# A cross-attention kernel: the softmax division leaves the probabilities and is done once per batch on the outputs

## The reference, cut to what matters

```python
def _L0_xattn_ref(query, context, Wq, bq, Wkv, bkv, Wout, bout):   # query (16, 64, 512), context (16, 1601, 512)
    q = query @ Wq + bq
    kv = context @ Wkv + bkv                       # interleaved k and v
    ...                                            # 16 heads of 32
    scores = jnp.einsum('bhid,bhjd->bhij', q, k) * SCALE
    attn = jax.nn.softmax(scores, axis=-1)
    out = jnp.einsum('bhij,bhjd->bhid', attn, v)
    return out.reshape(B, LQ, H * D) @ Wout + bout

x = x + _L0_xattn_ref(_layernorm(x), ctx_1024, ...)
x = x + _L0_attn_ref(_layernorm(x), ...)           # linear attention over the 64 rows of a batch
x = x + _L0_ffn_ref(_layernorm(x), ...)            # top 2 of 8 experts
```

## Time and profile before

| | us |
|---|---|
| median of 3 runs | 2648.12 |
| lowest and highest run | 2643.91, 2648.58 |
| the profiled execution: span from first to last instruction | 2643.8 |

### The profile page before, as it was taken

How to read it: one execution, slowest core, us unless ns; L and a number is a source line. 1 busy time by engine, 2 the same in 40 slices (tenths; PEclk the granted TensorE clock), 3 DMA queues, 4 the chain that set the end, 5 groups by cost and what they waited for, 6 DMA issues and landing times. The chain is left out here.

```text
span 2643.8 us, 41258 instructions
## 1 busy us (share of the span) xinstructions
PE 2413.4 (91%) x14596; PEld 2125.1 (80%) x14596; DVE 1749.9 (66%) x2316; ACT 1099.2 (42%) x1878; POOL 1081.5 (41%) x436
## 2 busy tenths in 40 slices
PE   8899999999999999999999999998579928999994
PEld 6688888888888888888888888886438628999993
DVE  3177777777778787777777777778764425554552
ACT  3244444444444454444444444444322214444440
POOL 2155555555455554545545555554320021111113
PEclk9999999999999999999999999999889959999997
DMA  4211111111111111111111111113030033443433
GB/s 149 90 29 45 37 45 41 54 43 38 38 49 43 35 57 37 38 52 33 53 45 37 39 46 54 39 42 102 8 142 1 1 123 136 148 157 141 167 123 119
DMA packets 114016, 176.91 MB, mean 67 GB/s; under 512 B 51856, under 2 KB 71568, under 8 KB 113808
## 3 DMA queue, kind: packets, MB, share of 16 engines
q1 hardware_dynamic: 108048, 159.51, 19.2%
q0 software_dynamic: 2560, 8.39, 1.0%
q10 hardware_dynamic: 3200, 6.29, 0.6%
HBM read 137.19 MB, written 36.96 MB: 66 GB/s over the span
## 5 line engine op out<-in xcount | busy, mean ns | idle before, releaser
L356 POOL TENSOR_TENSOR k_parts<-k_t,k_parts 64x1602 fp32r<-64x1602 f32 x128 | 426.0, 3328 | 458.1 <-DVE k_parts L418 458.0
L646 PE MATMUL ps_kv<-ctx_hi,wk_hi 128*128 128x256 f32 (+1 forms) x1536 | 464.0, 302 | 13.0 <-POOL ctx_lo L345 13.0
L646 PE MATMUL ps_kv<-ctx_lo,wk_hi 128*128 128x256 f32 (+1 forms) x1536 | 441.1, 287 | 0.0
L646 PE MATMUL ps_kv<-ctx_hi,wk_lo 128*128 128x256 f32 (+1 forms) x1536 | 440.6, 287 | 0.0
L370 POOL TENSOR_TENSOR v_parts<-v,v_parts 128x832 fp32r<-128x832 f32 x128 | 281.4, 2199 | 381.1 <-ACT v_parts L581 379.9
L451 DVE TENSOR_SCALAR probs_both<-probs_both,row_inv 128x1601 f32<-128x1601 f32 x128 | 407.4, 3183 | 4.5
L646 PE MATMUL ps_kv<-wv_hi,ctx_hi 128*128 128x512 f32 (+1 forms) x832 | 340.1, 409 | 0.0
L646 PE MATMUL ps_kv<-wv_hi,ctx_lo 128*128 128x512 f32 (+1 forms) x832 | 327.8, 394 | 0.0
L646 PE MATMUL ps_kv<-wv_lo,ctx_hi 128*128 128x512 f32 (+1 forms) x832 | 326.7, 393 | 0.0
L551 ACT ACTIVATE k_t<-ps_kv,bk_sb 128x256 f32<-128x256 f32 (+1 forms) x384 | 185.8, 484 | 306.3 <-PE ps_kv L646 301.7
L458 DVE TENSOR_TENSOR probs_t<-ps_pt,probs_t 128x512 fp32r<-128x512 f32 x368 | 205.9, 559 | 153.7 <-ACT probs_t L563 150.4
(11 more groups left out here) (215 smaller groups left out, 4219.2 us busy)
## 6 DMA issues: line engine op xcount, KB each, us to landing
w_raw<-w_dram SPq DMA_DIRECT2D x96, 512.0 KB, 4.8
ctx_raw<-ctx_dram SPq DMA_DIRECT2D x81, 512.0 KB, 3.6
rows_in<-zeros SPq DMA_DIRECT2D x90, 128.0 KB, 2.0
ctx_raw<-ctx_dram SPq DMA_DIRECT2D x16, 644.0 KB, 4.2
q_blocks<-q_parts SPq DMA_DIRECT2D x256, 32.0 KB, 1.8
rows_out<-zeros SPq DMA_DIRECT2D x1, 6144.0 KB, 21.2
rows<-rows_in SPq DMA_DIRECT2D x8, 768.0 KB, 5.7
rows_out<-down ACTq DMA_DIRECT2D x8, 768.0 KB, 3.6
```

The costliest lines, as they stand in the source:

```text
L356: nc.gpsimd.tensor_tensor(k_parts[64 - 64 * s:128 - 64 * s, :], k_t[par][64 * s:64 * s + 64, g, :], k_parts[64 * s:64 * s + 64, :].bitcast ...
L646: last = nc.tensor.matmul(o, still, moving, start=(k == 0 and i == 0), stop=(k == DT - 1 and i == 2))
```

## The change: what it does

- `normalise` is replaced by `invert`: DVE still takes the reciprocal of each row's sum, now kept for all eight pairs of a batch (`row_inv` is 128 x 2 x 8), and the multiplication of the 128x1601 probabilities is gone. Turn 0 waits for exp (`exp_done`) in place of the product.
- The outputs are then sums of undivided exponentials. `outputs` adds the four parts with one reduction over the lower 64 rows and two additions that read `ps_o` directly. `o_t` is 128 x 4 x 128: the pair's 64 rows by both heads' 64 columns; only the blocks in which head and rows agree are used. The turned and the values' matmuls now wait for `o_done`, the end of outputs, not for the reductions.
- Once per batch, at p = 0 of the next one, `divide` multiplies `o_t` by the inverse sums and adds the bias, two DVE operations of 128x512. The inverse sums stand as one number per partition (query), and are needed along the free axis: SP writes them to DRAM (`inv_t`, one transfer of single 4-byte elements), waits for it, and reads them back in four transfers that repeat each row over 32 partitions (`spread_inv`, at p = 7 behind `load_q`).
- The output is stored in four transfers in place of one (`store_o`), behind `o_final`.
- The score row stands centred in its four banks, at columns 222 to 1823: the column groups are 290, 512, 512 and 288 wide in place of 512, 512, 512 and 66.

```diff
@@ cross_attention, buffers
-        row_inv = sb("row_inv", [P, 2])
-        o_sum = sb("o_sum", [2 * HD, 2, P])
-        o_t = sb("o_t", [P, DT, LQ])
+        row_inv = sb("row_inv", [P, 2, PAIRS])
+        inv_rows = sb("inv_rows", [P, DT, LQ])
+        o_low = sb("o_low", [2 * HD, P])
+        o_mid = sb("o_mid", [2 * HD, P])
+        o_t = sb("o_t", [P, DT, P])
-        SC = [(c * BANK, min(BANK, LC2 - c * BANK)) for c in range(4)]
+        S0 = (4 * BANK - LC2) // 2 // 2 * 2
+        SC = [(max(c * BANK, S0), min((c + 1) * BANK, S0 + LC2)) for c in range(4)]
@@ SP
+            def store_o(b):
+                for s in range(2):
+                    for e in range(2):
+                        row = 2 * HD * s + HD * e
+                        to = attn_t.rearrange("(g p) n -> p g n", p=P)[row:row + HD, :, bass.ds(b * LQ, LQ)]
+                        sp.dma_start(to, o_t[row:row + HD, :, LQ * e:LQ * e + LQ]).then_inc(o_stored, 16)
+            def spread_inv(b, par):
+                sp.wait_ge(inv_done, PAIRS * (b + 1))
+                one = inv_t[bass.ds(b, 1)]
+                sp.dma_start(one.rearrange("a p e q -> (a e q) p"), row_inv[:, par, :],
+                             allow_slow_non_contiguous=True).then_inc(inv_stored, 16)
+                sp.wait_ge(inv_stored, 16 * (b + 1))
+                for s in range(2):
+                    for e in range(2):
+                        row = 2 * HD * s + HD * e
+                        src = one.rearrange("a (g s) e q -> s e (a g) q", s=2)[s, e]
+                        sp.dma_start(inv_rows[row:row + HD, :, :], src.unsqueeze(0).to_broadcast([HD, DT, LQ])
+                                     ).then_inc(inv_loaded, 16)
-                        sp.wait_ge(o_done, PAIRS * b)
-                        sp.dma_start(attn_t.rearrange(...)[:, :, bass.ds((b - 1) * LQ, LQ)], o_t[:]).then_inc(o_stored, 16)
+                        sp.wait_ge(o_final, b)
+                        store_o(b - 1)
+                    if p == PAIRS - 1:
+                        spread_inv(b, par)
@@ DVE, outputs
-                for part in range(2):
-                    nc.vector.tensor_reduce(o_sum[:, part, :], ps_o[64 * part:64 * part + 64, 0:2].rearrange("p h c -> p c h"),
-                                            AX.X, ALU.add).then_inc(o_halves, 1)
-                dve.wait_ge(o_halves, (n + 1) * 2)
-                for e in range(2):
-                    own = slice(HD * e, HD * e + HD)
-                    ins = nc.vector.scalar_tensor_tensor(
-                        out=o_t[64 * s + HD * e:64 * s + HD * e + HD, g, :], in0=o_sum[own, 0, LQ * e:LQ * e + LQ],
-                        scalar=bv_sb[own, p:p + 1], in1=o_sum[own, 1, LQ * e:LQ * e + LQ], op0=ALU.add, op1=ALU.add)
-                ins.then_inc(o_done, 1)
+                nc.vector.tensor_reduce(o_low[:], ps_o[64:128, 0:2].rearrange("p h c -> p c h"), AX.X, ALU.add
+                                        ).then_inc(o_low_done, 1)
+                dve.wait_ge(o_low_done, n + 1)
+                nc.vector.tensor_tensor(o_mid[:], ps_o[0:64, 0], o_low[:], ALU.add).then_inc(o_mid_done, 1)
+                dve.wait_ge(o_mid_done, n + 1)
+                nc.vector.tensor_tensor(o_t[64 * s:64 * s + 64, g, :], ps_o[0:64, 1], o_mid[:], ALU.add).then_inc(o_done, 1)
+            def divide(batches):
+                dve.wait_ge(o_done, PAIRS * batches)
+                dve.wait_ge(inv_loaded, 64 * batches)
+                rows_inv = inv_rows[:].unsqueeze(2).to_broadcast([P, DT, 2, LQ])
+                both = o_t[:].rearrange("p g (e q) -> p g e q", e=2)
+                nc.vector.tensor_tensor(both, both, rows_inv, ALU.mult).then_inc(o_scaled, 1)
+                dve.wait_ge(o_scaled, batches)
+                nc.vector.tensor_tensor(o_t[:], o_t[:], bv_sb[:].unsqueeze(2).to_broadcast([P, DT, P]), ALU.add
+                                        ).then_inc(o_final, 1)
@@ DVE, normalise -> invert
-                nc.vector.reciprocal(row_inv[:, q:q + 1], row_sum[:, q:q + 1]).then_inc(inv_done, 1)
-                dve.wait_ge(inv_done, n + 1)
-                nc.vector.tensor_scalar(probs[q], probs[q], row_inv[:, q:q + 1], None, ALU.mult
-                                        ).then_inc(probs_done, 1)
+                if p == 0 and positive(b - 1):
+                    dve.wait_ge(inv_stored, 16 * (b - 1))
+                nc.vector.reciprocal(row_inv[:, par, p:p + 1], row_sum[:, p % 2:p % 2 + 1]).then_inc(inv_done, 1)
@@ DVE, batch
                     if positive(n):
                         outputs(n - 1, (p - 1) % PAIRS)
+                        if p == 0:
+                            divide(b)
@@ PE, values and turn
-                    pe.wait_ge(o_halves, 2 * n)
+                    pe.wait_ge(o_done, n)
-                    pe.wait_ge(probs_done, n + 1)
+                    pe.wait_ge(exp_done, n + 1)
```

More of the change, by code:

```diff
@@ L533, in _ @@
             split_k(0, 0, 1)
-            normalise(0, 0)
+            invert(0, 0, 0, 0)
             over_batches(dve, batch)
             outputs(PAIRS * B - 1, PAIRS - 1)
+            divide(B)
         @block.scalar
```

42 lines of the change are left out of this document (21 added, 21 removed).

## The result

| | us |
|---|---|
| before, median of 4 runs beside the changed kernel | 2646.02 (2643.91 to 2648.58) |
| changed, median of 4 runs | 2584.94 (2578.70 to 2588.66) |
| ratio, 95% interval | 0.9763 (0.9746 to 0.9779) |
| span of the profiled execution, before and after | 2643.8 and 2584.5 |

The forecast was 2583 us. To see where the 59.3 us of the span went, each trace is cut at five marks: the start of the scores of the first pair, of the second, of the first pair of the last batch and of the last pair, and the first weight transfer of the next stage.

A forecast was written before the change was run, and what follows sets the result against it. PE was taken to bound the batches with units, a chain between engines the last batch. Terms -40, -3.5, -24 and +2.5 gave -65 us: span 2643.8 to 2579, median 2648.1 to 2583 us; 8-in-10 range 2557 to 2612.

The forecast's parts named there:

- Part 1: Batches with units: without the product, turn 0's 60 waits and the held-up STTs of p = 7 go; 40 us gained.
- The upper bound, 61.1: Most the batches with units could gain: weight loads' waits, 40.1 us for normalise plus 21.0 for the rest of a group.
- Part 2: `divide` at p = 0: its two DVE operations are hidden, price 0, margin about 1.5 us.
- the bound: `divide`: 5.8 us if both operations are held up by POOL as the STTs were; 1.4 us if neither is.
- Part 3: Inverse sums through DRAM: store lands in 4 us, loads at 1022.6, wanted at 1031.55; price 0, 9 us to spare.
- a landing under 6 us: Sign to look for in the changed kernel: the store of the inverse sums lands in under 6 us.
- Rival C: Slower: the 4-byte store lands late and holds up DVE at p = 0; 2760 us at a 25 us landing; chance 0.05.
- Part 4: Centred score row: PE at most 0.2 us faster per pair, but turn 3 waits for rest 2; price and gain 0.
- Part 5: First pair gains 3.5 us; last batch 24 us, as 7 pairs of 8.9 us; the end is 2.5 us slower.
- A: Centred score row pays after all, the scores' 0.2 us come out: 24 us more, 2559 us; chance 0.08.
- B: Freed time is lost at the next wait, turn 2 or turn 1, and in the last batch's chain: 2611 us; chance 0.12.
- D: Nothing changes, PE's waits at turn 0 were not normalise's: 2648 us; chance 0.03.

The follow-up runs named there:

- c11: Kernel before with only the new outputs sums that read `ps_o`, product and old division kept: 2634.56 us, ratio 0.9949; batches with units 1650.0 us.
- c2: Kernel before without the 128x1601 product, old outputs kept, division left out: batches with units 1646.9 us; whole time not comparable.
- c4: Changed kernel without the transfers of the inverse sums and the multiplication: batches with units 1618.6 us, last batch 64.2, end 17.8; whole time not comparable.
- c5: Changed kernel with two of the V unit's twelve matmuls moved ahead of turn 3: 2564.12 us, ratio 0.9685.
- c6: c5 with the score row back at column 0: 2580.90 us, ratio 0.9752.
- c1: Kernel before with the centred score row as its only edit: 2641.57 us, ratio 0.9972.
- c7: Changed kernel with the last batch's 6144 KB of zeros issued at p = 2, behind the output's store, not at p = 0: 2578.49 us, ratio 0.9741.
- c8: Changed kernel storing the inverse sums as one 32-byte piece per partition, so they end up misplaced: last batch 64.5 us, end 18.9; whole time not comparable.
- c9: Changed kernel storing the inverse sums of the first seven pairs ahead of `load_q`, pair 7's alone behind it: 2582.82 us, ratio 0.9748.
- c10: Changed kernel with the edits of c5, c7 and c9 together: 2553.07 us, ratio 0.9646.
- c12: Changed kernel with the edits of c5 and c7, inverse sums kept in query, pair order, moved in contiguous transfers: 2550.41 us, ratio 0.9624.

## Why the prediction was right, and where its sizes were off

**Part 1, mechanism right, term too small by 10.** Nothing took the product's place and the STTs' stall went. The term that was mis-sized is the 40 us, chosen by PE's idle time, where 50.5 came out: part of a wait is drawn as busy time (PE's busy time fell by 18 us), and the waits of the loads for rests came out whole, 18.5 us of waits for 19.0 us (c11). The upper bound, 61.1, held. The product's 40.1 us of waits are worth less, 22.1 alone (c2) and 30.8 with the sums already changed (1650.0 to 1619.2). The prediction spoke of these STTs as one stall at p = 7; without the new sums a second would have come.

**Part 2, right.** Hidden while there are units (c4), the multiplication held up in half of the batches for less than the bound. The addition ended before turn 0 in 14 of 15 batches and 0.4 us after its start in one, without cost, since DVE was idle for 1.6 us or more ahead of rest 0 in all of them.

**Part 3, outcome right by a small margin.** The store's landing, taken as 4 us and bounded by 5.6 from rows that had no 4-byte piece, took 7.9 to 10.3. Of the 9 us to spare at the batch shown, 0.8 were left. The prediction's own sign, a landing under 6 us, failed. Rival C's mechanism was real; it was cheap only because the chain that it stands on had slack, and that it had enough was in part luck. The two groups of the earlier trace rows were the wrong neighbours: what set the time was the size of the piece, not their number.

**Part 4, right.** Nil in this kernel, 17.4 us behind the wait that covers it (c5, c6), and 5.3 us in the kernel before (c1), which the reading of turn 3 alone did not show.

**Part 5.** The first pair came out (-3.4). In the last batch the last four pairs are the 8.3 to 8.9 us that were forecast; 8.5 us are missing against seven pairs of 8.9. 5.3 are the wait for the stores behind the zeros (c7), which no step of the prediction had (c4, c7 and c8 show it): of what is queued on SP behind `spread_inv` it named the context chunk and the store, not the zeros. 3.1 are the first of the seven (11.96 us; 11.94 before, 11.95 without the division): from its scores on PE still has the V unit and the last units of batch 14, so only six pairs are short, and seven were counted. The end costs 6.7 and not 2.5: the wait for the inverse sums was 5.2 us where up to 1 was put, which is part 3's mistake again. The granted clock between the cuts of the last batch rose from 0.80 to 0.88, for which the prediction had no term of its own; what that gave back is not shown.

**The sum.** The span was forecast at 2579 us and is 2584.5: 10.5 us too little in part 1, 12.9 too much in part 5, and 3.2 us at the start and behind the stage that have no term. The median came closer still, 2584.94 for 2583, since it lies 0.4 us over the span and 4.3 had been added. So two errors of over 10 us cancelled: that the forecast met the time to 2 us is luck, and what was right is the mechanism of parts 1, 2 and 4. Rivals A, B and D did not come, nor did C as a slower kernel. "The rest" moved by 2.4 us with no edited instruction; it took 727.6 to 733.1 us in the nine experiments that compute the right result, so 2.4 us are within its scatter.

## What to carry to other kernels

Look at which inputs of a DVE operation lie in SBUF before counting instructions: moving one input to PSUM was worth nearly as much in the batches with units (19.0 us) as removing an operation of 3.2 us a pair (22.1). When a wait vanishes, read what it covered: an edit worth nothing behind one wait (centring) is worth 17 us when two matmuls are moved ahead of the waiting one. For a small transfer that someone waits for, choose the layout in DRAM so that both sides move runs, and let the reading engine take the stride.

## What the runs showed of the hardware that was not expected

- A store of single 4-byte elements lands after 7.9 to 11.1 us (1024 elements) or 6.2 to 7.6 (128, in c9 and c10), the same 4 KB in pieces of 32 bytes after 1.1 to 1.5 (c8, c12). The elements' own packets had ended 1.2 to 1.3 us after the issue.
- A DVE operation of two SBUF inputs that began inside POOL's `k_parts` took 2.06 us in place of 0.69, and each that began inside an operation of POOL ended 0.07 us (32x64, before and c2) or 0.55 us (128x512, changed kernel) after it. With one input in PSUM none was stretched: in the changed kernel 120 of the 128 first sums began inside an operation of POOL and took at most 0.28 us.
- A multiplication of 128x512 of which one input's 4-byte numbers lie 32 bytes apart took DVE 1.08 to 1.15 us in c12, with adjacent ones 0.69.
- Four small stores behind one of 6144 KB on the same queue and 6 us behind it took 10.3 us to issue, against 1.8 when it had gone out 15.6 us before (c8).
